# A Mamba-style block with a ternary FFN on one core: the recurrence in sub-chunks of 64 tokens

## The reference

```python
x = x + mamba(layernorm(x)); x = x + ffn(layernorm(x))

def mamba(u):                                   # 8 heads of 64 channels, 16 states
    z0, x0, xBC, dt = split(u @ W_in.T)         # 512, 512, 512 + 16 + 16, 8 columns
    dt = softplus(dt + dt_bias);  A = -exp(A_log)
    xBC = silu(causal_conv(xBC, 4 taps) + conv_b);  x, B, C = split(xBC)
    for t: h = exp(dt_t * A) * h + dt_t * x_t * B_t;   y_t = h @ C_t + D * x_t
    y = layernorm(y) * ln_gamma + ln_beta
    y = sigmoid(y @ W_gate.T + b_gate) * y
    return concat(silu(z0) * x0, y) @ W_out.T

def ffn(x):                                     # 256 -> 1024 -> 256, weights in {-1, 0, 1}
    return layernorm(gelu(x @ ternary(W_fc))) @ ternary(W_proj)
```

## Time and profile before

| | before |
|---|---|
| median of 3 runs | 1097.28 us (1093.89 to 1099.71) |
| span of the profiled execution | 1095.2 us |
| TensorE busy | 1049.7 us, 96% |
| VectorE busy | 966.7 us, 88% |
| ScalarE busy | 962.1 us, 88% |
| GpSimd busy | 496.6 us, 45% |
| mean granted clock of TensorE | 0.991 |

### The profile page before, as it was taken

The page is one execution under the profiler, slowest core; times in us unless marked ns, Lnnn a source line. Parts: engine busy times, 40 slices in busy tenths (PEclk is TensorE's granted clock), DMA queues, the critical chain, the costliest instruction groups (busy, mean ns, idle before and its releaser), DMA issues.

```text
span 1095.2 us, 23188 instructions
## 1 busy us (share of the span) xinstructions
PE 1049.7 (96%) x8214; PEld 668.4 (61%) x8214; DVE 966.7 (88%) x2007; ACT 962.1 (88%) x1740; POOL 496.6 (45%) x590
## 2 busy tenths in 40 slices
PE   3877999999999999999999999999999999999997
PEld 1543756566575666657565665756666566666674
DVE  5998998999989999988999898899998988788766
ACT  5978698999999988899898999989899997989775
POOL 1543564353534544444434726443263733544552
PEclk9888999999999999999999999999999999999999
...
GB/s 199 203 12 39 100 76 78 50 98 116 98 91 95 50 126 98 107 97 96 72 78 116 103 121 87 89 95 62 117 97 113 87 80 63 117 78 64 115 124 161
DMA packets 306708, 105.94 MB, mean 97 GB/s; under 512 B 275488, under 2 KB 302880, under 8 KB 306592
## 3 DMA queue, kind: packets, MB, share of 16 engines
...
## 4 chain that ended last, share of the span: by engine, by line
PE 70%; DVE 11%; ACT 8%; issue 4%; DMA 3%; SPq 2%; POOL 1%; ACTq 0%; DVEq 0%; POOLq 0%
PE bank L399 44%; PE bank L634 8%; PE bank L622 7%; PE bank L560 3%; PE bank L569 2%; PE bank L475 2%; ACT L183 2%; DMA hT<-hb 2%; DVE cv L1018 2%; PE bank L521 1%; DVE EM L1138 1%; DVE st L981 1%; PE bank L545 1%; ACT EM L799 1%; DMA x<-in_x 1%
## 5 line engine op out<-in xcount | busy, mean ns | idle before, releaser
L399 PE MATMUL bank<-xnT,win 128*128 128x512 f16 (+1 forms) x1248 | 299.5, 387 | 19.6 <-DMA xnT<-hb 17.5
L399 PEld LDWEIGHTS bank<-xnT,win 128*128 128x128 f16 (+1 forms) x1248 | 122.2, 102 | 152.3 <-DVE win L930 17.5
L1018 DVE SCALAR_TENSOR_TENSOR cv<-bank,cws,cv 128x510 f32<-128x510 f32 (+5 forms) x240 | 177.4, 745 | 11.1 <-ACT tail L730 3.0
L399 PE MATMUL bank<-yhl,wg 128*128 128x512 f16 x768 | 173.0, 379 | 0.2
L1331 POOL TENSOR_TENSOR caty<-tg,caty 128x512 f16<-128x512 f32 x64 | 83.2, 1309 | 157.8 <-ACT caty L836 157.7
L183 ACT ACT_TABLE_LOAD x117 | 150.1, 1283 | 2.8 <-PEq L1526 0.7
L1326 POOL TENSOR_TENSOR yT<-yhl 128x512 f32<-128x512 f16 x64 | 79.6, 1265 | 113.8 <-DMA yhl<-ynh 113.8
L399 PEld LDWEIGHTS bank<-yhl,wg 128*128 128x128 f16 x768 | 74.3, 98 | 88.3 <-ACT EM L799 1.4
L1335 POOL TENSOR_TENSOR cat<-sz,cat 128x512 f16<-128x512 f32 x64 | 86.2, 1354 | 89.0 <-ACT cat L848 88.6
L634 PE MATMUL bank<-wpj,hT 128*128 128x256 f16 x1024 | 121.2, 273 | 5.2 <-DMA hT<-hb 5.2
L622 PE MATMUL bank<-wfc,x3T 128*128 128x512 f16 x512 | 122.2, 379 | 0.0
...
## 6 DMA issues: line engine op xcount, KB each, us to landing
...
crep<-cv SPq DMA_DIRECT2D x128, 32.0 KB, 2.0
hT<-hb SPq DMA_TRANSPOSE x128, 3.2
...
```

Source lines behind the costliest of these rows:

```text
L399: m = eng.matmul(b, lhs(p, k), rhs(q, k), start=(n == 0), stop=(n == len(seq) - 1))
L1018: op = eng.scalar_tensor_tensor(cs[0:w, j, 3 - k:T], b[0:w, 0:T - 3 + k], cws[0:w, j, k:k + 1], cs[0:w, j, 3 - k:T], ALU.mult, ALU.add)
```

## The change

The chunk stays at 128 tokens for sums and layouts, but the recurrence is taken over sub-chunks of 64: the state advances eight times per block (`advance`, nine buffers for five), and `own`, `gram`, `seg`, `exp_seg` and `mix` cover only the two 64x64 squares on each chunk's diagonal. `seg` has two units per block for four, `exp_seg` and `mix` handle four tiles of 512 for eight. `own` becomes 64 float32 matmuls of 64 columns over 64 rows, `carried` 64 of 64 columns over 32 rows, each head's rows of C being cleared for the other head (`c_grown` writes two versions of `ec`, and `state_mask` is gone), `states` 32 over 64 rows, `gram` 8 of 64 columns.

B, C and dt are projected in two column groups, tokens 0 to 255 on PSUM partitions 0 to 63 and tokens 256 to 511 on 64 to 127, six pairs of 256 and 259 columns and one matmul of 3 columns. Convolution, bias and SiLU take all of it in one instruction of 256 columns; dt's bias goes into the same bias. u and B are turned in two full transposes each. C goes to DRAM by two DMAs (`put_c`) and comes back by one that repeats it eight times. Block 0 is normalised and turned by TensorE (`turn_first`, X), split behind it, in place of four transposing DMAs. All five orders are new. A cut of the diff:

```diff
-    "c00 c01 c02 u03 v04 c05 c06 B07 z00 c13 m01 x02 x05 c10 x06 c14 z07 v02 u11 c15 g03701 x06 z03 s07 b00 c11 "
...
+    "X00 X01 c02 c03 z04 c05 c06 u07 c00 B01 v02 z03 c17 m05 x01 s06 c10 x04 g035 x01 u14 c17 b06 x00 c13 e05 c14 "
...
+            def turn_first(i, n, at):
...
+                for k in range(2):
+                    for c in range(2):
+                        at_t = (2 * k + c) * P
+                        m = eng.transpose(b[:, at_t:at_t + P], x[:, 2 * n + c, k * P:(k + 1) * P], ident)
...
-                wide, col = (104, BC0) if j == 4 else (P, XS0 + j * P)
-                products(b[0:wide, :], lambda p, k: win[:, p, k, col:col + wide], lambda q, k: xt[:, q, :, k, :],
-                         range(2)).then_inc(conv_mm, 1)
...
+                    seq = [(k, p, q) for k in range(2) for p, q in ((0, 0), (0, 1), (1, 0))]
+                    for m, (k, p, q) in enumerate(seq):
+                        w = win[:, p, k, BC0:BC0 + 64]
+                        eng.matmul(b[0:64, 3:259], w, xt[:, q, k, 0:256], start=(m == 0), stop=(m == 5))
+                        op = eng.matmul(b[64:128, 0:259], w, xt[:, q, k, 253:512], start=(m == 0), stop=(m == 5))
+                    op = eng.matmul(b[0:64, 0:3], win[:, 0, 0, BC0:BC0 + 64], none[:, 0:3], start=False, stop=True,
+                                    skip_group_check=True)
...
-                for c in range(NCH):
-                    m = eng.transpose(b[:, 8 * c:8 * c + 8], ucm[:, chunk(c)], ident[96:104, 96:104])
+                pe.wait_ge(taps, 5 * i + 1)
+                for q in range(2):
+                    m = eng.transpose(b[:, q * P:(q + 1) * P], bc[:, chunk(q)], ident)
...
-                    m = eng.matmul(hold[c][:, 0:P], bq[rows, :], crep[rows, chunk(c)], start=True, stop=True)
+                    for e in range(2):
+                        m = eng.matmul(hold[c // 2][rows(e), SUB * (c % 2):SUB * (c % 2) + SUB],
+                                       bcs[r, i % 2, sub(c % 2, e)], crep[r, sub(c, e)], start=True, stop=True)
...
+            def states(i, n, at0, at1):
+                hold = [take(at0), take(at1)]
                 for c in range(NCH):
-                    for j in range(4):
-                        m = eng.matmul(b[32 * j:32 * j + 32, chunk(c)],
-                                       BE[:, c, 2 * j:2 * j + 2, :].rearrange("p e n -> p (e n)"),
-                                       Xd[:, c, j * P:(j + 1) * P], start=True, stop=True)
+                    for e in range(2):
+                        for j in range(4):
+                            m = eng.matmul(hold[e][32 * j:32 * j + 32, chunk(c)],
+                                           BE[rows(e), c, 2 * j:2 * j + 2, :].rearrange("p e n -> p (e n)"),
+                                           Xd[rows(e), c, j * P:(j + 1) * P], start=True, stop=True)
                 m.then_inc(st_mm, 1)
...
-                    eng.matmul(b[:, :], segL[32 * c:32 * c + 27, i % 2, :],
-                               segR[32 * c:32 * c + 27, i % 2, hs, :].rearrange("p e t -> p (e t)"), start=True,
-                               stop=True).then_inc(seg_mm, 1)
...
+                for c in (2 * n, 2 * n + 1):
+                    for e in range(2):
+                        m = eng.matmul(hold[c % 2][rows(e), :], segL[32 * c:32 * c + 27, i % 2, rows(e)],
+                                       segR[32 * c:32 * c + 27, i % 2, :, rows(e)], start=True, stop=True)
...
-                for c in range(NCH):
-                    for j in range(4):
-                        m = eng.matmul(hold[j][:, chunk(c)], S[32 * j:32 * j + 32, (4 * i + c) % 5, :],
-                                       ec[32 * j:32 * j + 32, chunk(c)], start=(c == 0), stop=False,
-                                       skip_group_check=True)
+                for k in range(2 * NCH):
+                    for e in range(2):
+                        for j in range(4):
+                            m = eng.matmul(hold[j][rows(e), sub(0, k)], S[32 * j:32 * j + 32, (8 * i + k) % 9, rows(e)],
+                                           ec[32 * j:32 * j + 32, e, sub(0, k)], start=(k == 0), stop=False,
+                                           skip_group_check=True)
...
             def own(i, n):
-                p, half = UNITS[n]
                 hold = bank["r", i, 0]
-                pe.wait_ge(em, 4 * i + n + 1)
-                for c in (2 * p, 2 * p + 1):
-                    for j in (2 * half, 2 * half + 1):
+                half, swap = n // 2, (0, 1, 1, 0)[n]
+                pe.wait_ge(em, 2 * i + half + 1)
+                if n % 2:
+                    pe.wait_ge(own_mm, 4 * i + n)
+                for c in (2 * half, 2 * half + 1):
+                    for g in range(2):
                         for e in range(2):
-                            at = j * P + 64 * e
-                            m = eng.matmul(hold[j][64 * e:64 * e + 64, chunk(c)], Xd[:, c, at:at + 64],
-                                           EM[:, c % 2, 4 * (n % 2) + 2 * (j % 2) + e, :], start=False, stop=True,
-                                           skip_group_check=True)
+                            for h_ in range(2):
+                                j = 2 * ((h_ + swap) % 2) + g
+                                at = j * P + 64 * e
+                                m = eng.matmul(hold[j][rows(e), sub(c, h_)], Xd[rows(h_), c, at:at + 64],
+                                               EM[rows(h_), c, 2 * j + e, :], start=False, stop=True,
+                                               skip_group_check=True)
...
+                    eng.activation(xnT[:, 0, 0, :, 256 * n:256 * n + 256], b[:, :].rearrange("p (k t) -> p k t", k=2),
+                                   ACT.Copy).then_inc(xn_hi, 1)
...
+                    op = eng.activation(bc[:, :], b[:, 3:259], ACT.Identity, scale=cws[:, 4, 3:4], bias=sm("cb")[:, 4:5])
...
-                eng.activation(cs[64:80, 4, :], cs[32:48, 4, :], ACT.Silu).then_inc(c_act, 1)
-                eng.activation(bcu[64:80, :], cs[0:16, 4, :], ACT.Silu).then_inc(b_act, 1)
-                act.wait_ge(ld_const, 16)
-                for c in range(NCH):
-                    op = eng.activation(bq[32 * c:32 * c + 16, :], cs[0:16, 4, chunk(c)], ACT.Silu)
...
+                eng.activation(bcs[:, i % 2, :], bc[:, :], ACT.Silu).then_inc(bc_act, 1)
...
-                    act.wait_ge(seg_mm, 8 * i + 2 * n + c + 1)
-                    act.wait_ge(own_mm, 4 * i + n - 1)
-                    eng.activation(EM[:, c, es, :].rearrange("p e t -> p (e t)"), bank["q", i, n][c][:, :], ACT.Exp
+                    eng.activation(EM[:, 2 * n + c, :, :].rearrange("p e t -> p (e t)"), bank["q", i, n][c][:, :], ACT.Exp
                                    ).then_inc(e_exp, 1)
...
+                    if j == 4:
+                        op = eng.scalar_tensor_tensor(bc[:, :], b[:, k:k + 256], cws[:, 4, k:k + 1], bc[:, :], ALU.mult,
+                                                      ALU.add)
...
-                then(eng.tensor_copy(dec[:, :], ec[:, :].rearrange("p (c t) -> p c t", c=NCH)[:, :, P - 1]))
...
-                eng.tensor_tensor(ec[:, :], crep[:, :], ec[:, :], ALU.mult).then_inc(ce, 1)
+                then(eng.scalar_tensor_tensor(ec[:, 1, :], crep[:, :], of_head[1], ec[:, 0, :], ALU.mult, ALU.mult))
+                eng.scalar_tensor_tensor(ec[:, 0, :], crep[:, :], of_head[0], ec[:, 0, :], ALU.mult, ALU.mult
+                                         ).then_inc(ce, 1)
...
-                for c in range(NCH):
-                    at = 4 * i + c
-                    op = eng.scalar_tensor_tensor(S[:, (at + 1) % 5, :], S[:, at % 5, :], dec[:, c:c + 1], bum[:, c, :],
-                                                  ALU.mult, ALU.add)
-                    if c < 3:
+                for k in range(2 * NCH):
+                    at = 8 * i + k
+                    op = eng.scalar_tensor_tensor(S[:, (at + 1) % 9, :], S[:, at % 9, :], dec[:, k:k + 1],
+                                                  hold[k % 2][:, chunk(k // 2)], ALU.mult, ALU.add)
+                    if k < 7:
...
             def mix(i, n):
-                p, _ = UNITS[n]
-                es = slice(4 * (n % 2), 4 * (n % 2) + 4)
-                dve.wait_ge(gm, 4 * i + 2 * p + 2)
-                for c in range(2):
-                    dve.wait_ge(e_exp, 8 * i + 2 * n + c + 1)
-                    op = eng.scalar_tensor_tensor(EM[:, c, es, :], EM[:, c, es, :], 1.0,
-                                                  Gm[:, 2 * p + c, :].unsqueeze(1).broadcast_to([P, 4, P]), ALU.min,
-                                                  ALU.mult)
+                dve.wait_ge(gm, 2 * i + n + 1)
+                for c in (2 * n, 2 * n + 1):
+                    dve.wait_ge(e_exp, 4 * i + c + 1)
+                    op = eng.scalar_tensor_tensor(EM[:, c, :, :], EM[:, c, :, :], 1.0,
```

(13 more changed lines are left out.)

310 lines of the change are left out of this document (175 added, 135 removed), and 236 rows, old and new, of tables (ACT_ORDER, DVE_ORDER, PE_ORDER, POOL_ORDER).

## The result

The changed kernel takes 1121.3 us (median of 4 runs, 1117.0 to 1125.6), the kernel before, run beside it, 1098.5: a ratio of 1.0228 (95% interval 1.0205 to 1.0251; the two medians alone give 1.0208), 2.3% slower where the prediction had 3.4% faster. The profiled execution is the longest of the four, with a span of 1123.8 us; it is 28.6 us longer than that of the kernel before, while the medians differ by 22.8, so accounts made from the two traces hold some 6 us that belong to the single execution.

The account below looks back on a forecast made before the run. TensorE's own work was taken to bound nearly all of the span, VectorE the stretch from 50 to 100 us. 1095.2 - 31.6 - 2.6 - 4 + 1.5 = 1058.5 us span, so 1060 us, 3.4% faster; range 1044 to 1104.

Parts of the forecast that it names:

- every wait priced at nothing: Steady stretch: waits priced at nothing beyond today's, upper bound 2 us a block; VectorE about -34 us, keeping its slack.
- the cover is gone: Rival: with TensorE quicker, waits that are nil today cost 1 to 2 us a block, 1076 to 1090 us; chance 0.14.
- TensorE's own work: Sum of TensorE's terms over 16 blocks, including layout changes and block 0's turn: -31.6 us.
- own and its layout changes: Local part of the recurrence: 32 steps of 0.058 us for 0.109, -26.2 us; layout changes of all groups, +2.9.
- projection: B/C/dt projection: six steps of 0.109 us in two column groups side by side, 0.68 for 1.30 a block, -9.8 us.
- C times B: L510: grows by 0.18 us a block on its busier tiles, its second half starting behind the first, +2.9 us.
- block 0's turn with its wait: Turning block 0 on TensorE at the start: 8 transposes, +0.9 us.
- carried: Carried states (L545): 8 steps of 0.112 us become 16 steps of eight tiles at 0.058, +0.5 us.
- records do not start closer: Rival: 28 ns a record as floor in carried, own and states, about 1143 us (1128 at 25 ns); chance 0.13.
- the second rival: Column tiles in the same rows share loads, or 64-column steps cost as much as 128: about 1103 us; chance 0.08.
- C over DRAM: SyncE issues 3 transfers for C in place of 8, each later by one DRAM trip; nothing gained.
- The first 100 us: Start: TensorE's chain ready at about 14.9 us, -2.6; relief from 50 to 100, -4; TensorE's saving unseen there, +1.5.

Follow-up runs that it names:

- GpSimd light: Changed kernel with three of GpSimd's 512-column products cut to 128 columns from block 1 on, the rest stale: 0.9994 of the kernel before.
- the kernel with the small records: Kernel before with 64 tiny matmuls a block (128 records, 8 columns moving) ahead of carried: 1.0324 of the kernel before.
- the wrong place: Kernel before with C written to DRAM by one transfer and spread by another, a store and a transpose between them in SyncE's queue: 1.0117.
- all suspects off: Changed kernel with 64 wide records in carried, four advance steps and the second C pass left out, three GpSimd products cut to 128 columns: 0.9863 of the kernel before.
- carried's wide form: Changed kernel with each head pair in carried sharing one matmul of 128 weight columns, 64 records for 128, heads mixed: 1.0161 of the kernel before.
- VectorE's shorter chain: Changed kernel without four of the eight advance steps and the second pass over C on VectorE: 1.0147 of the kernel before.

## Why the prediction was wrong, step by step

**The step that failed** is the sentence "Both engines thus keep at least the slack of the earlier trace rows, and the saving of TensorE is not handed over to them", and with it every wait priced at nothing. VectorE's sum was made of new counts times durations of the kernel before, and those durations hold for the meetings with GpSimd that the old order happened to have. In place of the slack the runs showed VectorE 981.4 us busy, TensorE idle for 40.0 of the 950 us from 100 to 1050 (5.0 before), and 28.2 us of TensorE's waits over the whole span on VectorE (12.5 before). With GpSimd's instructions cut short, the kernel was 26 us faster. The sum by instructions was fair: with GpSimd light VectorE is 931.5 us busy, forecast about 930. But even then TensorE idles 21.0 us from 100 to 1050, so the waits would not have been nothing either; 11.2 us of the idle time of that run stand on "issue", for which the prediction has no term. The time above 1106 us had a chance of 0.13 there, by a floor under the distance of records; it came about, but not by that floor. The rival that named the outcome's kind, "the cover is gone" (1076 to 1090), had the place right and the size too small: it asked which waits the new steps make, not whether the steps that stay still last as long. GpSimd does not appear in the prediction at all, though the earlier trace rows has it 45% busy.

The Trainium skill states the rule, in "SBUF — State Buffer", section "SBUF: two separate sides": VectorE and GpSimd share a pair of ports under an exclusive lock. A VectorE instruction that is in a two-port mode, or that has two inputs in SBUF while GpSimd's instruction reads SBUF, and the GpSimd instruction block each other; the one that starts first keeps the ports for its whole length. The trace agrees where two inputs are concerned: the advance, whose second input now stands in PSUM, has no long instruction left (330 to 349 ns over all 128, for up to 1343 before), and the masked product, with two inputs in SBUF, reaches 1651. For the 26 long ones with a single input the profile does not show the mode.

**TensorE's own work** was to fall by 31.6 us. Adding the starts of its records with every run at the median of its kind, it fell by 14.8 (1023.8 to 1009.0; with the runs grouped otherwise, by 13.2). By terms: own and its layout changes -21.5 (forecast -26.2 and +2.9); projection -8.4 (-9.8); C times B -0.4 (+2.9); decay differences -2.1 (-1.8); turns of u and B -3.4 (-1); states +1.2 (0); block 0's turn with its wait +4.0 (+0.9); **carried +8.4 (+0.5)**, the worst sized of the terms; and some 7 in the feed-forward matmuls, which have no term of their own and which the new order cuts into more runs (164 groups for 125). The forecast of own at 14 to 15 ns a record held to the nanosecond, because weights and moving columns both had 64 columns. Carried's step was taken from own's 0.058. Some groups of eight records do start 0.058 us apart, most take 0.066 to 0.168: 7 to 9 ns a record in places, 16 to 17 in others, 11 on average.

The rival "records do not start closer" was wrong in its number: the floor of about 25 ns that it takes from the Trainium skill ("TensorE: Matmul & The Clock Gate", section "Wait — 56ns, not 53.3ns?") is beaten by own over 32 records, at 14.7 ns each. It was right that small records have a limit of their own: some 10 ns over 128 nearly empty records and 11 in carried, for the 7 that the forecast took, and gaps of 0.4 to 3.4 us when dense runs follow each other. That the gaps are a matter of supply the landing times of the instruction packets show; for the spacing it is only likely. On the gaps the Trainium skill says, in "Runtime: NRT & Kernel Launch", section "Instruction fetch mechanics", that instructions are fetched in blocks of 256 ahead of their use, and that the cost of a block is mostly hidden. The trace agrees for most of the 91 instruction packets of the changed kernel (65 before), but not for eight of them: all eight gaps within own and carried, 9.1 us idle in all, end 1.4 to 1.5 us after a packet has landed, as the seven in the kernel with the small records do. Column tiles sharing their loads (the second rival) did not happen: the projection's pairs start within 10 ns.

**C over DRAM**: "Nothing is gained there, since no engine waits for SyncE's queue now" was true of before and not of after. The trip is free, as priced (1.0007); its place in the queue is not (about 4 us here, 12 to 13 in the kernel before with the wrong place).

**The first 100 us.** TensorE's first matmul comes at 10.3 us, and the projection, which the forecast meant, at 14.28 (forecast 14.9). But little of it is left at 100 us: after its first matmul TensorE idles 21.8 us of the first 100, for 15.0 before. It waits 3.6 us for block 1's transposing DMAs at 34.1 and 4.1 us for ScalarE at 56.5, its granted clock from 25 to 50 is 0.80 for 0.93, and from 50 to 100 VectorE leads (47.84 of 50 us) and its relief did not come. The stretch from 25 to 50, before and after:

```profile
25.00:50.00 25.00, 23.76 (x140) 13.60 (x137) 23.60 (x53) 22.71 (x40) 15.23 (x21) 0.93 0.62 186
```

```profile
25.00:50.00 25.00, 19.75 (x131) 12.40 (x138) 20.05 (x47) 16.55 (x30) 8.15 (x15) 0.80 0.51 113
```

**The account.** Start 17.5 to 10.3, -7.2; own work -14.8; what is left, idle time and slow clock, +50.6, of which 35 is TensorE's idle time from 100 to 1050 and 9 its idle time elsewhere behind the start: together +28.6, the difference of the spans. Of the 40 us between the changed kernel and the one with all suspects off, GpSimd alone gives 26, carried's wide form 7 and VectorE's shorter chain 9, these two together 23; the effects overlap, and how much of each one owns is not a single number.
